# Attention with split values: one product for both halves of v, and part of a weight rounding moved to GpSimd

## The chip, the cores and the metric

The kernel runs on one core of a Trainium2 chip. The metric is the device time of one execution in microseconds (us). Five engines work side by side, each through its own program in order, and wait for each other on semaphores: TensorE (PE, with its weight loads as PEld), VectorE (DVE), ScalarE (ACT), GpSimd (POOL) and SyncE (SP), which issues the transfers.

## What is computed

The reference is one decoder layer on x of shape (16, 256, 512), in three parts, each added to x: attention with 16 heads of width 32, a gated long convolution, and a feed-forward part with weights rounded to 8-bit floats. Cut to what the change touches:

```python
qkv = _bitlinear(layernorm(x), w_qkv)              # int8-like activations, ternary weights
attn = softmax(where(causal, q @ k.T * SCALE, NEG))
out = einsum('bhnm,bmhd->bnhd', attn, v)
x = x + _bitlinear(out, w_proj)                    # out is rounded per row before the product
...
wq = w.astype(float8_e4m3fn).astype(x.dtype)       # gate_w and up_w, 512 x 1536 each
```

## The kernel before, in words

The first part of the program is attention. 16 batches of 8 pairs of heads make 128 pairs, numbered n = 8 b + p. All engines walk the same list of steps t (`STEPS`), and each has its own share of a step, so that pair n is in a different phase on each engine at one time. In step t:

- TensorE first does `weigh(t - 12)` (the product of probabilities and values, L509 to L512), then `row_max(t)` (scores for the row maximum, into the one tile `s_qk`, from L457), then `probabilities(t - 8)` (scores again, into `s_kq`, L478 to L492), and then what projections and transposes are due in that step.
- VectorE first does `take_max(t - 1)` (L802, reads `s_qk`), then now and then `high_part` (L826), `finish` (L834, L838, L844, L847, L852), `scale_qk` (L782), `split_v` (L792, L795), the layer norm's pieces, and last `weight_pieces`.
- ScalarE copies `weigh`'s result out of PSUM into `oraw` (L1216), takes the exponentials (L1202), splits off the high half `pH` (L1208), and rounds.
- GpSimd makes the low half `pL` of the probabilities (L1458), the low halves of q and k (L1451), and its part of `weight_pieces` (L1470, L1473).

There is a single `s_qk`: `row_max(n)` on TensorE waits for `take_max(n - 1)` on VectorE, and `take_max(n)` waits for `row_max(n)`. `pv`, the tile that `weigh` fills, is single too and is freed by ScalarE's copy; `pL` has two buffers, freed by `weigh`.

For precision, probabilities p and values v are each split into two f16 numbers, high and low. A pair has 2 heads and 3 blocks of 128 x 128 each (two on the diagonal, one below). For each block `weigh` issues four products: pH with vH, pH with vL, pL with vL, pL with vH. vH has 33 columns a head (32 values and a column of ones, which gives the softmax sum), vL has 32, and all four add into the same 33 columns of `pv`. That is 24 products a pair, each with a weight load of its own.

Once a batch, `finish` in its step k = 0 takes the reciprocal of the sums (L834) and multiplies `oraw` by it into `o_sb` (L838). Its later steps round and project `o_sb` and add to x.

Beside attention, the 24 pieces (128 x 512) of the gate and up weights are rounded to 8-bit floats, one piece in every five steps. With t % 5 == 1 VectorE masks the exponent of a piece (L865) and turns it into the rounding constant (L867: bound below, then factor), while GpSimd finishes the piece before (L1470). With t % 5 == 0, four steps after the masking, GpSimd adds the constant to the piece (L1473) and VectorE takes a maximum (L871).

After the last pair, the steps run on until the last batch is finished (the tail), x goes through DRAM, and the second part (convolution and feed-forward) begins.

Of the kernel before, what the change touches and what calls it, by code (L numbers as in the profile page):

```python
# [5 lines left out]
F32 = mybir.dt.float32  # L6
F16 = mybir.dt.float16
# [6 lines left out]
P = 128  # L14
# [52 lines left out]
def decoder_kernel(nc, x, skip, ctx_in, w_qkv, w_proj, k_turned, w_gate, w_up, w_down,  # L67
# [23 lines left out]
    with ExitStack() as ctx:  # L91
        def sb(where, name, shape, dt):
            return where.enter_context(nc.sbuf_tensor(name, shape, dt))
# [16 lines left out]
        wmax = sb(ctx, "wmax", [P, 2, CB * INNER // PIECE], F32)  # L110
        cols = sb(ctx, "cols", [P, 2 * IB + M_HEADS], F32)
        gs, us, skips = cols[:, 0:IB], cols[:, IB:2 * IB], cols[:, 2 * IB:]
        rows_s = sb(ctx, "rows_s", [2 * IB, P], F32)
        rows_k = sb(ctx, "rows_k", [M_HEADS, M_POS], F32)
        rows_kb = sb(ctx, "rows_kb", [M_HEADS, B, M_POS], F32)
        same_seq = sb(ctx, "same_seq", [P, B, M_POS], F32)
        GROUP = 4
        ws = sb(ctx, "ws", [P, 8], F32)
# [30 lines left out]
        with ExitStack() as prep:  # L149
            wraw = [sb(prep, f"wraw{i}", [P, WB, C], F32) for i in range(4)]  # L150
            tern = [sb(prep, f"tern{i}", [P, WB, C], BF16) for i in range(2)]
            wsums = sb(prep, "wsums", [P, 4], F32)
        packs.append(q("pack2", [P, 2, R, GQ, N], F16))
        oraw = [q(f"oraw{i}", [P, NT, HEADS, VW], F32) for i in range(2)]
        fw_raw = [q(f"fw_raw{i}", [P, PIECE], F32) for i in range(3)]
        fw_pow = [q(f"fw_pow{i}", [P, PIECE], F32) for i in range(2)]
        o_sb = q("o_sb", [P, NT, C + 1], F32)
        fw_out = [q(f"fw_out{i}", [P, PIECE], F16) for i in range(2)]
        vH = [q(f"vH{i}", [P, NT, HEADS, VW], F16) for i in range(3)]
        vL = [q(f"vL{i}", [P, NT, HEADS, D], F16) for i in range(3)]  # L160
        blockmax = [q(f"blockmax{i}", [P, PAIRS, 6], F32) for i in range(2)]
        negmax = [q(f"negmax{i}", [P, NT, 32], F32) for i in range(2)]
        nmT = [q(f"nmT{i}", [P, N], BF16) for i in range(2)]
# [226 lines left out]
        def tensor_program(tensor):  # L390
# [103 lines left out]

            def weigh(n):
                b, p = divmod(n, PAIRS)
                ph, pl, vh, vl = pH[n % NP], pL[n % 2], vH[b % 3], vL[b % 3]
                acc = pv[:, 0:NT * 2 * VW].rearrange("p (t h w) -> p t h w", t=NT, h=2)
                w.wait_ge(*high_done(n))
                w.wait_ge(low_done, n + 1)  # L500
                w.wait_ge(v_high, 2 * b + 2)
                w.wait_ge(v_low, 2 * b + 2)
                w.wait_ge(const_done, C_ONCE)
                w.wait_ge(pv_out, n)
                for t in range(NT):
                    for hh in range(2):
                        for mt in range(t + 1):
                            block, h = 2 * hh + t if mt == t else 4 + hh, 2 * p + hh
                            T.matmul(acc[:, t, hh, :], ph[:, block, :], vh[:, mt, h, :], start=mt == 0, stop=False)  # L509
                            T.matmul(acc[:, t, hh, 0:D], ph[:, block, :], vl[:, mt, h, :], start=False, stop=False)  # L510
                            T.matmul(acc[:, t, hh, 0:D], pl[:, block, :], vl[:, mt, h, :], start=False, stop=False)
                            made = T.matmul(acc[:, t, hh, :], pl[:, block, :], vh[:, mt, h, :], start=False, stop=mt == t)  # L512
                made.then_inc(pv_pe, 1)

            def turn_oq(b, j):
# [202 lines left out]
        def vector_program(vector):  # L718
# [66 lines left out]
            def split_v(b, t):  # L785
                n, bank = 2 * b + t, misc1.of["v", b, t]
                w.wait_ge(v_pe, n + 1)
                w.wait_ge(c_done, b + 1)
                w.wait_ge(const_done, C_ONCE)
                if b >= 3:  # L790
                    w.wait_ge(pv_pe, PAIRS * (b - 2))
                V.tensor_scalar(vH[b % 3][:, t, :, 0:D], bank[:].rearrange("p (h d) -> p h d", h=HEADS),  # L792
                                small[b % 4][:, 12 + t:13 + t], None, ALU.mult).then_inc(v_high, 1)
                w.wait_ge(v_high, n + 1)
                V.scalar_tensor_tensor(out=vL[b % 3][:, t], in0=bank[:].rearrange("p (h d) -> p h d", h=HEADS),  # L795
                                       scalar=small[b % 4][:, 12 + t:13 + t], in1=vH[b % 3][:, t, :, 0:D],
                                       op0=ALU.mult, op1=ALU.subtract).then_inc(v_low, 1)

            def take_max(n):
# [28 lines left out]
            def finish(b, k):  # L828
# [3 lines left out]
                if k == 0:  # L832
                    w.wait_ge(pv_out, PAIRS * (b + 1))
                    chain.step(V.reciprocal(rl, oraw[b % 2][:, :, :, D]))  # L834
                    chain.wait()
                    if b > 0:
                        w.wait_ge(oqT_pe, 2 * b)
                    V.tensor_tensor(o_sb[:, :, 0:C].rearrange("p t (h d) -> p t h d", d=D), oraw[b % 2][:, :, :, 0:D], rl.unsqueeze(3).broadcast_to([P, NT, HEADS, D]),  # L838
                                    ALU.mult).then_inc(o_mult, 1)
                elif k == 1:  # L840
                    w.wait_ge(o_mult, b + 1)
                    if b >= 2:
                        w.wait_ge(ostep_done, b - 1)
                    V.tensor_reduce(out=am, in_=o_sb[:], op=ALU.max, axis=AXIS.X, apply_absolute_value=True).then_inc(omax_done, 1)  # L844
                elif k == 2:
                    w.wait_ge(ostep_done, b + 1)
                    V.reciprocal(inv, step).then_inc(oscale_done, 1)  # L847
                elif k in (10, 12):
                    t, xs = (k - 10) // 2, x_sb[b % NX]
                    w.wait_ge(proj_pe, 2 * b + t + 1)  # L850
                    w.wait_ge(c2_done, b + 1)
                    V.scalar_tensor_tensor(out=xs[:, t, :], in0=misc1.of["proj", b, t][:], scalar=c2[:, t:t + 1],  # L852
                                           in1=xs[:, t, :], op0=ALU.mult, op1=ALU.add).then_inc(x1_done, 1)

            def weight_pieces(k):
# [3 lines left out]
                if not second and n < PIECES:  # L859
# [2 lines left out]
                    w.wait_ge(fw_in[n % 3], 16 * (n // 3 + 1))  # L862
                    if n >= 2:
                        w.wait_ge(fw_taken, n - 1)
                    chain.step(V.tensor_scalar(pw[:].bitcast(I32), raw[:].bitcast(I32), EXPONENT, None, ALU.bitwise_and))  # L865
                    chain.wait()
                    V.tensor_scalar(pw[:], pw[:], FP8_MIN_NORMAL, FP8_STEP, ALU.max, ALU.mult).then_inc(fw_pow_done, 1)  # L867
                if second and n > 0:
                    m, at = divmod(n - 1, PIECES // 2)
                    w.wait_ge(fw_taken, n)  # L870
# [247 lines left out]
        def scalar_program(scalar):  # L1118
# [90 lines left out]

            def weighed(n):  # L1210
                b, p = divmod(n, PAIRS)
                acc = pv[:, 0:NT * 2 * VW].rearrange("p (t h w) -> p t h w", t=NT, h=2)
                w.wait_ge(pv_pe, n + 1)
                if b >= 2:
                    w.wait_ge(o_mult, b - 1)
# [184 lines left out]
        def gpsimd_program(gpsimd):  # L1400
# [59 lines left out]
            def weight_pieces(k):  # L1460
# [9 lines left out]
                    G.tensor_tensor(fw_out[i % 2][:], fw_raw[i % 3][:], fw_pow[i % 2][:], ALU.subtract).then_inc(fw_taken, 1)  # L1470
                if second and n < PIECES:
                    w.wait_ge(fw_pow_done, n + 1)
                    G.tensor_tensor(fw_raw[n % 3][:], fw_raw[n % 3][:], fw_pow[n % 2][:], ALU.add).then_inc(fw_added, 1)  # L1473

            power_in(0)
# [6 lines left out]
            for i in range(2):  # L1482
                G.memset(nmT[i][:], 0.0).then_inc(const_done, 1)
            for i in range(3):
                G.memset(vH[i][:, :, :, D:VW], 1.0).then_inc(const_done, 1)
            for t in STEPS:
                if (n := pair(t, LOW)) is not None:
                    low_part(n)
# [287 lines left out]
```

## Time and profile before

| what | value |
|---|---|
| median of 3 runs | 1677.63 us (1677.42 to 1678.31) |
| profiled execution | 1676.79 us |
| its span in the trace | 1675.1 us |
| TensorE busy | 1545.5 us (92%) |
| VectorE busy | 1251.7 us (75%) |
| GpSimd busy | 929.1 us (55%) |
| ScalarE busy | 666.0 us (40%) |

The profiled execution is 1.7 us longer than its span and 0.8 us shorter than the median of the runs. The busy shares are averages over parts with different limits: the attention loop takes from 93 us (first `weigh`) to 504 us (last `row_max`) of the span, its tail until about 547 us, the second part the rest. Busy time of TensorE counts each product until its result has drained, so products that follow each other closely overlap in it: starts of products say more than their durations.

### The profile page before, as it was taken

The page shows a single profiled execution, that of the slowest core. Times are in us where ns is not written, and L with a number is a line of the kernel's source. Part 1 is how long each engine was busy: PE and PEld are TensorE (multiplying, and loading weights), DVE is VectorE, ACT ScalarE, POOL GpSimd, SP SyncE. Part 2 cuts the span into 40 slices and gives each one's busy share as a digit, 9 for nine tenths or more (in the row PEclk, how much of TensorE's full clock was granted, in tenths as well). Part 3 has the DMA queues.
Part 4 walks back from the last instruction along what each step waited for, and adds up shares of the span by engine and source line. Part 5 has one row for each costly group of instructions (what it writes and reads, how often), then busy time and mean ns, then how long its engine had stood idle before and what let it go on. Part 6 is the DMA issues. An engine that isn't in the chain of part 4 may idle for free.

```text
span 1675.1 us, 27334 instructions
## 1 busy us (share of the span) xinstructions
PE 1545.5 (92%) x10646; PEld 884.8 (53%) x10646; DVE 1251.7 (75%) x1866; ACT 666.0 (40%) x1190; POOL 929.1 (55%) x677
## 2 busy tenths in 40 slices
PE   2698999999897878899999999999999999999998
PEld 2477777777775333444444444444444444444443
DVE  6799898889883879877777777777776877777521
ACT  4578777777666101322222322222223222232131
POOL 3388788778764455744554545534653454355242
PEclk9799999999998899999999999999999999999999
DMA  3653645545341513010200210020020021010000
GB/s 127 156 135 107 166 108 138 132 114 147 83 112 53 156 44 88 20 32 1 70 26 7 52 38 13 19 70 13 13 76 13 7 64 32 1 45 1 1 26 26
DMA packets 61953, 105.87 MB, mean 63 GB/s; under 512 B 7912, under 2 KB 14080, under 8 KB 61824
## 3 DMA queue, kind: packets, MB, share of 16 engines
q1 hardware_dynamic: 61728, 104.10, 23.5%
q8 instruction: 85, 1.39, 0.3%
q14 instruction: 44, 0.36, 0.1%
q10 hardware_dynamic: 96, 0.01, 0.0%
HBM read 50.61 MB, written 19.92 MB: 42 GB/s over the span
## 4 chain that ended last, share of the span: by engine, by line
PE 75%; DVE 14%; issue 5%; ACT 3%; POOL 1%; DMA 1%; SPq 1%; POOLq 0%; DVEq 0%; ACTq 0%
PE gu L675 20%; PE y L640 11%; PE gu L689 9%; PE gu L628 3%; PE y L643 3%; PE y L648 3%; PE y L647 3%; PE y L644 3%; PE y L646 3%; DVE blockmax L802 3%; PE misc L603 1%; PE s_kq L478 1%; DVE fw_pow L865 1%; PE misc L445 1%; PE misc L436 1%
## 5 line engine op out<-in xcount | busy, mean ns | idle before, releaser
L1539 POOL TENSOR_TENSOR fuL<-fu,fuH 128x512 f16<-128x512 f32 x96 | 116.2, 1210 | 305.5 <-ACT fuH L1356 305.5
L1458 POOL TENSOR_TENSOR pL<-pT,pH 128x768 f16<-128x768 f32 x128 | 220.3, 1723 | 88.5 <-PE pv L512 38.9
L640 PE MATMUL y<-kv,toep 128*128 128x512 f32 x496 | 238.3, 601 | 7.1 <-DVE z L989 6.7
L1000 DVE TENSOR_REDUCE oT<-z 128x64 f32<-128x512 f32 x256 | 175.7, 686 | 8.8
L675 PE MATMUL gu<-fT,wg 128*128 128x512 f16 x768 | 181.4, 379 | 0.0
L675 PE MATMUL gu<-fT,wu 128*128 128x512 f16 x768 | 181.4, 379 | 0.0
L1202 ACT ACTIVATE pT<-s_kq,ws 128x768 f32<-128x768 f32 x128 | 115.3, 901 | 104.1 <-PE s_kq L492 104.1
L1356 ACT ACTIVATE fuH<-fu 128x512 f16<-128x512 f32 x96 | 60.2, 627 | 240.0 <-DVE fu L1016 240.0
L993 DVE TENSOR_TENSOR z<-y,shared 128x512 f32<-128x512 f32 x112 | 77.1, 688 | 95.0 <-PE y L644 60.1
L689 PE MATMUL gu<-wd,fuH 128*128 128x512 f16 x384 | 145.5, 379 | 0.0
L689 PE MATMUL gu<-wd,fuL 128*128 128x512 f16 x384 | 145.5, 379 | 0.0
L1518 POOL TENSOR_TENSOR kv<-vT,cT 128x1024 f32<-128x1024 f32 x64 | 138.5, 2184 | 6.2 <-ACT vT L1333 6.2
L675 PEld LDWEIGHTS gu<-fT,wg 128*128 128x128 f16 x768 | 75.0, 98 | 119.1 <-issue 47.1
L640 PEld LDWEIGHTS y<-kv,toep 128*128 128x128 f32 x496 | 91.5, 192 | 86.9 <-issue 60.0
L996 DVE TENSOR_TENSOR z<-z,cT 128x512 f32<-128x512 f32 x112 | 129.0, 1151 | 3.8
L675 PEld LDWEIGHTS gu<-fT,wu 128*128 128x128 f16 x768 | 75.1, 98 | 106.4 <-issue 35.4
L802 DVE TENSOR_REDUCE blockmax<-s_qk 128x6 f32<-128x768 f32 x128 | 121.4, 948 | 12.0 <-PE s_qk L462 11.7
L1339 ACT ACTIVATE shared<-gu 128x512 f32<-128x512 f32 x56 | 33.4, 597 | 217.1 <-PE gu L628 217.1
L989 DVE TENSOR_TENSOR z<-y,cT 128x512 f32<-128x512 f32 x144 | 98.5, 684 | 28.4 <-PE y L640 28.4
L1451 POOL TENSOR_TENSOR qkhl<-qkt,qkhl 128x512 f16<-128x512 f32 x64 | 80.0, 1252 | 38.5 <-ACT qkhl L1188 38.4
L478 PE MATMUL s_kq<-pack 128*128 128x128 f16 x768 | 100.6, 221 | 0.0
L1016 DVE SCALAR_TENSOR_TENSOR fu<-gu,cols,sil 128x512 f32<-128x512 f32 x96 | 71.5, 745 | 37.6 <-PE gu L675 36.4
(196 smaller groups left out, 3802.0 us busy)
## 6 DMA issues: line engine op xcount, KB each, us to landing
pack<-qkhl SPq DMA_DIRECT2D x256, 128.0 KB, 2.7
x_sb<-in_x SPq DMA_DIRECT2D x16, 512.0 KB, 4.8
c_sb<-in_ctx SPq DMA_DIRECT2D x32, 256.0 KB, 3.9
hankel<-in_L_xattn_k SPq DMA_DIRECT2D x32, 256.0 KB, 4.9
x_grp<-x_scratch SPq DMA_DIRECT2D x32, 256.0 KB, 3.9
out_y<-yo SPq DMA_DIRECT2D x32, 256.0 KB, 2.8
x_scratch<-x_sb SPq DMA_DIRECT2D x15, 512.0 KB, 3.0
wraw<-in_L_attn_w_qkv SPq DMA_DIRECT2D x3, 1024.0 KB, 8.7
```

Of the source, the lines that this page charges most:

```text
L478: T.matmul(to, pack[:, 1, r, g, key * P:(key + 1) * P], pack[:, 0, r, g, query * P:(query + 1) * P], start=first, stop=False)
L640: made = T.matmul(to, tap(h, lb - kb), keys_values(h, kb, half), start=kb == 0, stop=kb == lb)
L675: made = T.matmul(bank[:], (wg, wu)[which][:, cb, ib * P:(ib + 1) * P], fT[:, cb, part, :], start=cb == 0 and part == 0, stop=cb == CB - 1 ...
L689: made = T.matmul(bank[:], src[:, ib, t * P:(t + 1) * P], wd[:, ib, :], start=ib == 0 and part == 0, stop=ib == IB - 1 and part == 1)
L802: V.tensor_reduce(out=blockmax[b % 2][:, p, :], in_=s_qk[:, 0:6, :], op=ALU.max, axis=AXIS.X, negate=True).then_inc(max_done, 1)
L989: V.tensor_tensor(z[n % 2][:], y, weight, ALU.mult).then_inc(m_zm, 1)
L996: chain.step(V.tensor_tensor(z[n % 2][:], z[n % 2][:], weight, ALU.mult))
L1000: V.tensor_reduce(out=oT[h % 2][:, lb, own].rearrange("p (b j) -> p b j", b=HB), in_=z[n % 2][:], op=ALU.add, axis=AXIS.X).then_inc(m_z, 1)
L1202: S.activation(pT[n % NP][:], s_kq[:, 0:6, :], ACT.Exp, scale=ws[:, 4:5]).then_inc(exp_done, 1)
L1458: G.tensor_tensor(pL[n % 2][:], pT[n % NP][:], pH[n % NP][:], ALU.subtract).then_inc(low_done, 1)
L1518: G.tensor_tensor(kv[LB * (h % 2) + lb][:], vT[h % 2][:, lb, :].rearrange("p (b i) -> p b i", b=B).unsqueeze(2).broadcast_to([P, B, M_POS, ...
L1539: G.tensor_tensor(fuL[:, ib, :], fu[n % 2][:], fuH[:, ib, :], ALU.subtract).then_inc(f_fl, 1)
```

## The change

vH and vL become one tile `vHL` with 65 columns a head: 32 high values, the column of ones, 32 low values. `weigh` issues two products a block instead of four: pH with all 65 columns, pL with all 65 columns, into 65 columns of `pv`. ScalarE's copy into `oraw` takes 260 elements instead of 132. `finish` adds the last 32 columns of each head to the first 32, once a batch, between the reciprocal and the multiplication. The second step of the weight pieces' constant (L867) goes from VectorE to GpSimd, where it stands ahead of the addition L1473. Three small tiles move into a region of memory that is used again later.

```diff
-        oraw = [q(f"oraw{i}", [P, NT, HEADS, VW], F32) for i in range(2)]
+        oraw = [q(f"oraw{i}", [P, NT, HEADS, VW + D], F32) for i in range(2)]
-        vH = [q(f"vH{i}", [P, NT, HEADS, VW], F16) for i in range(3)]
-        vL = [q(f"vL{i}", [P, NT, HEADS, D], F16) for i in range(3)]
+        vHL = [q(f"vHL{i}", [P, NT, HEADS, VW + D], F16) for i in range(3)]
...
-                            T.matmul(acc[:, t, hh, :], ph[:, block, :], vh[:, mt, h, :], start=mt == 0, stop=False)
-                            T.matmul(acc[:, t, hh, 0:D], ph[:, block, :], vl[:, mt, h, :], start=False, stop=False)
-                            T.matmul(acc[:, t, hh, 0:D], pl[:, block, :], vl[:, mt, h, :], start=False, stop=False)
-                            made = T.matmul(acc[:, t, hh, :], pl[:, block, :], vh[:, mt, h, :], start=False, stop=mt == t)
+                            T.matmul(acc[:, t, hh, :], ph[:, block, :], v[:, mt, h, :], start=mt == 0, stop=False)
+                            made = T.matmul(acc[:, t, hh, :], pl[:, block, :], v[:, mt, h, :], start=False, stop=mt == t)
...
                     chain.step(V.reciprocal(rl, oraw[b % 2][:, :, :, D]))
+                    chain.step(V.tensor_tensor(oraw[b % 2][:, :, :, 0:D], oraw[b % 2][:, :, :, 0:D], oraw[b % 2][:, :, :, VW:VW + D],
+                                               ALU.add))
                     chain.wait()
...
-                    chain.step(V.tensor_scalar(pw[:].bitcast(I32), raw[:].bitcast(I32), EXPONENT, None, ALU.bitwise_and))
-                    chain.wait()
-                    V.tensor_scalar(pw[:], pw[:], FP8_MIN_NORMAL, FP8_STEP, ALU.max, ALU.mult).then_inc(fw_pow_done, 1)
+                    V.tensor_scalar(pw[:].bitcast(I32), raw[:].bitcast(I32), EXPONENT, None, ALU.bitwise_and).then_inc(fw_pow_done, 1)
...
                     w.wait_ge(fw_pow_done, n + 1)
+                    chain.step(G.tensor_scalar(fw_pow[n % 2][:], fw_pow[n % 2][:], FP8_MIN_NORMAL, FP8_STEP, ALU.max, ALU.mult))
+                    chain.wait()
                     G.tensor_tensor(fw_raw[n % 3][:], fw_raw[n % 3][:], fw_pow[n % 2][:], ALU.add).then_inc(fw_added, 1)
```

## Rows read from the trace of the kernel before

**Rows 1.** The page: span of the profiled execution.

```profile
span 1675.1 us, 27334 instructions
```

**Rows 2.** Stretches: PE, PEld, DVE, ACT, POOL busy us, then granted clock.

```profile
93.00:504.00 411.00, 373.91 (x5677) 312.15 (x5676) 367.31 (x557) 307.72 (x620) 329.50 (x235) 0.98 0.48 123
504.00:547.00 43.00, 29.82 (x445) 21.39 (x443) 15.19 (x23) 25.15 (x49) 18.24 (x11) 0.85 0.20 66
...
700.00:1675.00 975.00, 967.62 (x3808) 457.18 (x3806) 675.44 (x985) 257.64 (x397) 458.51 (x316) 1.00 0.10 28
```

**Rows 3.** Who waited for whom, 93 to 505 us: total us, times, longest.

```profile
PE s_qk L457 <- DVE blockmax L802: 32.9, 26, 2.6
...
DVE vH L792 <- PE misc L445: 13.0, 19, 0.8
```

**Rows 4.** TensorE in order of time around 325 us: start us, us, engine, line.

```profile
324.24 0.22 PE L478 MATMUL s_kq<-pack 128*128 128x128 f16 x1
...
324.35 0.22 PE L478 MATMUL s_kq<-pack 128*128 128x128 f16 x1
...
325.34 0.18 PE L509 MATMUL pv<-vH,pH 128*128 128x33 f16 x1
...
325.92 0.18 PE L512 MATMUL pv<-vH,pL 128*128 128x33 f16 x1
```

**Rows 5.** VectorE groups by line, 90 to 533 us: count, busy us, mean ns.

```profile
L867 DVE TENSOR_SCALAR fw_pow<-fw_pow 128x512 f32<-128x512 f32 x22 | 27.5, 1252 | 0.8
...
L838 DVE TENSOR_TENSOR o_sb<-oraw,osmall 128x1024 f32<-128x1024 f32 x16 | 24.2, 1515 | 0.8 <-PE misc L521 0.3
```

**Rows 6.** VectorE L838 alone: min/median/max ns.

```profile
L838 DVE TENSOR_TENSOR o_sb<-oraw,osmall x16: 1226/1253/2299, 122.9 to 532.0; 128x1024 f32<-128x1024 f32 x16
```

**Rows 7.** What TensorE waited for before L509: us, times.

```profile
  POOL pL L1458: 0.5, 1
```

**Rows 8.** GpSimd in order of time around 320 us.

```profile
319.99 1.65 POOL L1458 TENSOR_TENSOR pL<-pT,pH 128x768 f16<-128x768 f32 x1 [0.26 <-PE pv L512]
```

**Rows 9.** GpSimd's part of the rounding: min/median/max ns.

```profile
L1473 POOL TENSOR_TENSOR fw_raw<-fw_raw,fw_pow x24: 1265/1275/1287, 69.1 to 483.4; 128x512 f32<-128x512 f32 x24
```

**Rows 10.** ScalarE copies out of PSUM, 132 and 256 elements: min/median/max ns.

```profile
L1216 ACT ACTIVATE oraw<-pv x128: 253/272/322, 94.7 to 531.0; 128x132 f32<-128x132 f32 x128
...
L1160 ACT ACTIVATE cbc<-misc x16: 375/376/384, 25.6 to 435.1; 128x256 f32<-128x256 f32 x16
```

**Rows 11.** TensorE in order of time: L457 of pairs 68 to 72.

```profile
293.01 0.38 PE L457 MATMUL s_qk<-pack 128*128 128x256 f16 x2
...
295.91 0.38 PE L457 MATMUL s_qk<-pack 128*128 128x256 f16 x2
...
299.04 0.38 PE L457 MATMUL s_qk<-pack 128*128 128x256 f16 x2
...
302.81 0.38 PE L457 MATMUL s_qk<-pack 128*128 128x256 f16 x2
...
308.16 0.41 PE L457 MATMUL s_qk<-pack 128*128 128x256 f16 x2 [2.29 <-DVE blockmax L802]
```

**Rows 12.** VectorE in order of time, the same stretch.

```profile
294.49 0.95 DVE L802 TENSOR_REDUCE blockmax<-s_qk 128x6 f32<-128x768 f32 x1
...
297.55 0.94 DVE L802 TENSOR_REDUCE blockmax<-s_qk 128x6 f32<-128x768 f32 x1
...
301.19 0.95 DVE L802 TENSOR_REDUCE blockmax<-s_qk 128x6 f32<-128x768 f32 x1
...
305.49 1.75 DVE L867 TENSOR_SCALAR fw_pow<-fw_pow 128x512 f32<-128x512 f32 x1
307.16 0.94 DVE L802 TENSOR_REDUCE blockmax<-s_qk 128x6 f32<-128x768 f32 x1
```

**Rows 13.** TensorE in order of time: L457 of pairs 42 and 82.

```profile
199.09 0.39 PE L457 MATMUL s_qk<-pack 128*128 128x256 f16 x2 [1.41 <-DVE blockmax L802]
...
346.00 0.39 PE L457 MATMUL s_qk<-pack 128*128 128x256 f16 x2 [1.42 <-DVE blockmax L802]
```

More of the change, by code:

```diff
@@ L112, in decoder_kernel @@
         gs, us, skips = cols[:, 0:IB], cols[:, IB:2 * IB], cols[:, 2 * IB:]
-        rows_s = sb(ctx, "rows_s", [2 * IB, P], F32)
-        rows_k = sb(ctx, "rows_k", [M_HEADS, M_POS], F32)
-        rows_kb = sb(ctx, "rows_kb", [M_HEADS, B, M_POS], F32)
         same_seq = sb(ctx, "same_seq", [P, B, M_POS], F32)
@@ L152, in decoder_kernel @@
             wsums = sb(prep, "wsums", [P, 4], F32)
+            rows_s = sb(prep, "rows_s", [2 * IB, P], F32)
+            rows_k = sb(prep, "rows_k", [M_HEADS, M_POS], F32)
+            rows_kb = sb(prep, "rows_kb", [M_HEADS, B, M_POS], F32)
         packs.append(q("pack2", [P, 2, R, GQ, N], F16))
-        oraw = [q(f"oraw{i}", [P, NT, HEADS, VW], F32) for i in range(2)]
+        oraw = [q(f"oraw{i}", [P, NT, HEADS, VW + D], F32) for i in range(2)]
         fw_raw = [q(f"fw_raw{i}", [P, PIECE], F32) for i in range(3)]
@@ L496, in weigh @@
                 b, p = divmod(n, PAIRS)
-                ph, pl, vh, vl = pH[n % NP], pL[n % 2], vH[b % 3], vL[b % 3]
-                acc = pv[:, 0:NT * 2 * VW].rearrange("p (t h w) -> p t h w", t=NT, h=2)
+                ph, pl, v = pH[n % NP], pL[n % 2], vHL[b % 3]
+                acc = pv[:, 0:NT * 2 * (VW + D)].rearrange("p (t h w) -> p t h w", t=NT, h=2)
                 w.wait_ge(*high_done(n))
@@ L791, in split_v @@
                     w.wait_ge(pv_pe, PAIRS * (b - 2))
-                V.tensor_scalar(vH[b % 3][:, t, :, 0:D], bank[:].rearrange("p (h d) -> p h d", h=HEADS),
+                V.tensor_scalar(vHL[b % 3][:, t, :, 0:D], bank[:].rearrange("p (h d) -> p h d", h=HEADS),
                                 small[b % 4][:, 12 + t:13 + t], None, ALU.mult).then_inc(v_high, 1)
                 w.wait_ge(v_high, n + 1)
-                V.scalar_tensor_tensor(out=vL[b % 3][:, t], in0=bank[:].rearrange("p (h d) -> p h d", h=HEADS),
-                                       scalar=small[b % 4][:, 12 + t:13 + t], in1=vH[b % 3][:, t, :, 0:D],
+                V.scalar_tensor_tensor(out=vHL[b % 3][:, t, :, VW:VW + D], in0=bank[:].rearrange("p (h d) -> p h d", h=HEADS),
+                                       scalar=small[b % 4][:, 12 + t:13 + t], in1=vHL[b % 3][:, t, :, 0:D],
                                        op0=ALU.mult, op1=ALU.subtract).then_inc(v_low, 1)
@@ L1211, in weighed @@
                 b, p = divmod(n, PAIRS)
-                acc = pv[:, 0:NT * 2 * VW].rearrange("p (t h w) -> p t h w", t=NT, h=2)
+                acc = pv[:, 0:NT * 2 * (VW + D)].rearrange("p (t h w) -> p t h w", t=NT, h=2)
                 w.wait_ge(pv_pe, n + 1)
@@ L1484, in gpsimd_program @@
             for i in range(3):
-                G.memset(vH[i][:, :, :, D:VW], 1.0).then_inc(const_done, 1)
+                G.memset(vHL[i][:, :, :, D:VW], 1.0).then_inc(const_done, 1)
             for t in STEPS:
```

## The prediction

> **What bounds the kernel now.** I read the page first for the span [rows 1], then the busy time of each engine in four stretches [rows 2]. The change touches only attention and the weight rounding beside it, so only the loop (93 to 504 us) and its tail count; of the second part the reader should see that TensorE is busy 967.6 of 975 us, and nothing of it is edited. I take it as unchanged: whatever attention gains or loses passes to the end in full.
>
> In the loop no engine is full: TensorE 373.9, VectorE 367.3, GpSimd 329.5 and ScalarE 307.7 of 411 us. The third view, who waited for whom, says how the first two share the time [rows 3]: TensorE's scores (L457) waited 32.9 us in 26 places for VectorE's maximum (L802), since there is one `s_qk`, while VectorE's own largest wait for TensorE is the 13.0 us ahead of L792. So the limit alternates. In most of the steps TensorE runs without a gap, in about a quarter VectorE is late and TensorE stands. A gain on one engine is worth something only in its own steps.
>
> **TensorE's part.** The 24 products of a pair start from 325.34 to 325.92, with 23 intervals between them: 25 ns each, 0.605 us a pair [rows 4]. The change issues 12. The trace has no 65-column product. Bounds: no cheaper than the 33 columns' 25 ns (12 x 25 = 0.30 us), no dearer than 128 columns, where two products take from 324.24 to 324.35, 55 ns each [rows 4] (12 x 55 = 0.66 us, slightly more than now). Per column the 128-column row gives 0.43 ns, so 65 columns want 28 ns; I take 28, since 25 ns at 33 columns lies above that line and so looks like a floor that 65 columns only just pass. 12 x 28 = 0.34 us: TensorE saves 0.27 us a pair, and could save 0.30 or lose 0.05.
>
> The Trainium skill, "TensorE: Matmul & The Clock Gate", section "Back-to-back issue gap", speaks against this: it gives a sustained spacing of about 81 ns a product at 128 columns for a stream of weight load and product, because both set the pace. If 65 columns cost that, a pair would take 0.97 us instead of 0.605, an estimate from that page. The trace has 55 ns there, so I go by the trace; the rule is taken up below as a rival.
>
> The first twelve steps of scores have no `weigh` beside them; 116 pairs have both. If TensorE alone set the time, 116 x 0.27 = 31 us would go.
>
> **VectorE's part.** Removed: L867, mean 1.25 us in the loop [rows 5], 24 of them, 30 us. That is far more than the instruction's own work must be, but it stands in VectorE's queue all the same. Added: 16 additions, of the shape of L838 (1024 elements, two inputs in SBUF): 1.23 us at least, 1.52 on the mean, 2.30 at most [rows 5, 6]. I take 1.23 plus 0.04 for the chained wait in the walk below, and charge the difference to the mean, 0.29, separately. 16 x 1.5 = 24 us. So VectorE's total hardly changes (30 off, 24 on); what changes is in which steps it stands. The removed piece lies in steps n % 5 == 1, VectorE's longest, where TensorE's waits are. The added piece lies in the step where a batch finishes. Behind it on VectorE stand L838, L782 and the next L802, for which TensorE waits.
>
> **Both together, step by step.** Two facts of the rows make a walk possible [rows 11, 12]: a released L457 starts 1.00 us after the L802 it waited for (307.16 to 308.16), and otherwise follows its own queue. Write P for TensorE's own work between two L457 and D for VectorE's between two L802. Pairs 68 to 72, before: P = 2.90, 3.13, 3.77, and 5.35 less the 2.29 that it waited and the 0.15 by which a product's drain (0.18) outlasts the next start, so 2.91; D = 3.06 (with L838), 3.64, 5.97 (with L867 at 1.75) [rows 11, 12]. After: each P less 0.27; the first D plus 1.27, the last less 1.75: 4.33, 3.64, 4.22. Start both as they stand, L457 of pair 68 at 0, L802 at 1.48:
>
> - pair 69: L457 at 2.63, L802 at 5.81.
> - pair 70: L457 at max(5.49, 6.81) = 6.81 (a new wait of 1.3), L802 at 9.45.
> - pair 71: L457 at max(10.31, 10.45) = 10.45, L802 at 13.67.
> - pair 72: L457 at max(13.09, 14.67) = 14.67 (a wait of 1.5, before 2.29).
>
> Before it was 15.15: four steps give 0.5 us where TensorE alone saves 1.1. The addition takes back what the removal gives. The pattern of batches (8 steps) and pieces (5 steps) repeats after 40 pairs, from pair 42 at 199.09 to pair 82 at 346.00, 146.9 us [rows 13]. Walked in the same way, its eight groups of five give 0.8, 2.5, 0.5, 1.0, 0.9, 1.1, 1.2 and -0.3 us: 7.7 us. The groups with a finish give 0.6 on the mean, those without 1.5. In steps with `split_v` the saving is also partly lost, as VectorE waits there for TensorE's v, and the shorter `weigh` comes after it. For 116 pairs: 116 / 40 x 7.7 = 22 us.
>
> **What is taken off this.** Additions that meet GpSimd work: 15 in the loop at 0.29 more, 4 us, of which I count 3, since some of these steps have slack. The tail: ScalarE is busy 25.2 of 43 us there, and has the exponentials and copies in a row. Its copy grows from 132 to 260 elements, 272 to 376 ns by the 256-element row [rows 10], 0.1 us a pair: hidden in the loop (ScalarE idles 103 us there), 1.2 us in the tail's 12 steps. The last batch's addition has no cover, since everything waits for `o_sb`: 1.3 us. No instruction and no transfer is added to SP's queue.
>
> **GpSimd's part.** Added: 24 times one 128 x 512 instruction. The trace has no such instruction with a single input. The two-input one of that size, 1.28 us [rows 9], is the upper bound; VectorE's L867 at its mean, 1.25, is no better. A gain is excluded, as work is only added, so the lower end is zero; I take 1.0, near the upper row, 24 us in all, or 350 of 390 us busy. What covers it: `pL` is ready early. The one that the `weigh` at 325.34 uses ended at 319.99 + 1.65 = 321.64, 3.7 us ahead [rows 4, 8], and TensorE waited for `pL` once in the whole execution, 0.5 us [rows 7]. Four steps lie between VectorE's masking and GpSimd's use of it, so the new place makes nobody wait. Cost 0. With that cover gone (less than 1 us of lead left) each piece could stop TensorE by up to 1.28, 31 us.
>
> Sum: 22 - 3 - 1.2 - 1.3 = 16.5 us off the profiled 1676.8, 1660.3; the median stands 0.8 higher, so **1661 us**.
>
> **Rivals.** First, *the freed time comes out nearly whole*: VectorE's waits for TensorE shrink with `weigh`, and the walk charges the addition too high. For it: the removed L867 sits where TensorE waits. Against: the walk. 31 - 2.5 = 29 us, 1648.
>
> Second, *the addition takes it all*: it meets GpSimd instructions as the longest L838 did, at 2.30, nearly every time, now that GpSimd is fuller. 15 x 1.1 = 16 us against the 3 that I charged, a gain of 4: about 1673, or no measurable change. For it: 2.30 exists. Against: the median is 1.25 [rows 6].
>
> Third, the other side, *the wide product is dear*. Its place is TensorE in `weigh`, its price the spacing of 65-column products with a weight load each; TensorE loses from 50 ns a product on. At 55 ns it costs 116 x 0.05 = 6 us, which the removal of L867 about balances (24 waits shortened by a part of 1.25, 16 lengthened). At 75 ns it would be 12 x 75 - 605 = 0.3 us a pair, 34 us, less some 5: 1706. For it speaks only that two instructions issue per product; against it the 55 ns at 128 columns. By the page's 81 ns it would be 0.37 a pair, some 43 us, near 1715.
>
> **How the numbers follow.** A measurement of this kernel can tell about 0.2%, 3.4 us, from no change. Forecast (1653 to 1669): 0.60. Nearly whole gain (1645 to 1653): 0.19. Addition takes it: 0.17, of which 0.07 is no measurable change. Wide product dear: 0.04. Faster 0.60 + 0.19 + 0.10 = 0.89, same 0.07, slower 0.04. The range goes from 1646 to 1672: the lower end holds most of the second case with 0.30 us a pair, the upper the larger half of the third.
>
> **What would show it.** Right: 12 products a pair from first to last in 0.3 to 0.35 us; the loop's 411 us become about 393; TensorE's waits for L802 stay at some 25 to 35 us, but some stand behind the steps with a finish; the addition at 1.2 to 1.6 us; the tail 2 us longer; the second part as long as before. Wrong: products more than 40 ns apart, waits of TensorE for `pL` of more than a few us, additions near 2.3, or TensorE's waits falling below 15 us (then the gain is larger).

## The result and the profile after

The changed kernel takes 1686.72 us (median of 4 runs, 1685.04 to 1687.05), the kernel before 1677.97 on the same chip: a ratio of 1.0049, 95% interval 1.0032 to 1.0067. It is slower by 8.7 us; 1661 was predicted. One execution of a later kernel, the one with the multiplication moved, took 2052.81 us at a granted clock of 0.74, in a slower state of the chip, and is left out of its median. Page and stretches of the changed kernel (columns as in [rows 2]; the loop is cut from the row maximum of pair 12 to that of pair 127, the second stretch ends at the first product of the second part):

```profile
span 1683.2 us, 24212 instructions
```

```profile
95.00:507.60 412.60, 349.41 (x4192) 282.14 (x4249) 372.15 (x544) 317.74 (x616) 383.44 (x256) 0.97 0.47 121
507.60:555.70 48.10, 27.39 (x297) 19.21 (x300) 20.07 (x28) 27.31 (x50) 18.76 (x12) 0.85 0.22 70
555.70:1683.20 1127.50, 1097.22 (x4172) 515.89 (x4172) 803.73 (x1182) 285.60 (x438) 544.34 (x376) 0.99 0.13 34
```

The same three stretches of the kernel before:

```profile
97.00:504.00 407.00, 371.21 (x5631) 309.79 (x5630) 363.35 (x552) 305.65 (x616) 327.24 (x233) 0.98 0.48 122
504.00:549.40 45.40, 29.82 (x445) 21.40 (x444) 15.81 (x27) 25.96 (x50) 18.80 (x12) 0.83 0.24 74
549.40:1675.00 1125.60, 1094.49 (x4172) 514.35 (x4172) 803.94 (x1182) 285.58 (x438) 544.82 (x376) 0.99 0.13 34
```

The ramp before the loop became 2.0 us shorter, the loop 5.6 longer, the tail 2.7 longer, the second part 1.9 longer: together, but for rounding, the 8.1 us between the spans. Why the ramp and the second part changed by 2 us each is not shown. In the loop TensorE is busy 22 us less, as intended. VectorE is busy 8.8 us more, although it was meant to lose as much as it gained, and GpSimd 56 us more.

Where this comes from. TensorE's products, in order of time:

```profile
322.24 0.19 PE L509 MATMUL pv<-vHL,pH 128*128 128x65 f16 x1
322.27 0.20 PE L510 MATMUL pv<-vHL,pL 128*128 128x65 f16 x1
...
322.61 0.38 PE L457 MATMUL s_qk<-pack 128*128 128x256 f16 x2
```

Twelve products in 0.37 us, 31 ns each, where 24 had started 25 ns apart [rows 4]: the price was nearly right. VectorE's finish and GpSimd's rounding, minimum, median and maximum in ns:

```profile
L833 DVE TENSOR_TENSOR oraw<-oraw x16: 1160/1514/2454, 121.1 to 535.4; 128x1024 f32<-128x1024 f32 x16
L838 DVE TENSOR_TENSOR o_sb<-oraw,osmall x16: 1227/2547/2556, 123.2 to 536.6; 128x1024 f32<-128x1024 f32 x16
```

```profile
L1471 POOL TENSOR_SCALAR fw_pow<-fw_pow x24: 1917/1922/2782, 68.6 to 483.6; 128x512 f32<-128x512 f32 x24
L1473 POOL TENSOR_TENSOR fw_raw<-fw_raw,fw_pow x24: 1261/1272/1452, 70.7 to 485.6; 128x512 f32<-128x512 f32 x24
```

The addition's median is 1.51 us, and L838, which the change does not touch, went from a median of 1.25 [rows 6] to 2.55. GpSimd's new instruction takes 1.92 us, more than the two-input instruction of the same size that was my upper bound [rows 9]. The waits between 93 and 505 us, where [rows 3] had 32.9 us for TensorE:

```profile
ACT pT L1200 <- POOL pL L1456: 43.3, 32, 2.9
...
PE s_qk L457 <- DVE blockmax L800: 35.6, 25, 3.5
PEld pv L509 <- issue: 29.5, 46, 2.8
```

TensorE waits for VectorE as long as before, although VectorE has lost L867, and ScalarE now waits 43.3 us for `pL`, for which only TensorE had waited, once, before [rows 7]: an exponential needs a `pT` that GpSimd has read. The last line, in which the profile names no releaser, hides a wait of the same kind. In 16 places of attention TensorE stands for more than 0.3 us, 13.9 us together, and then starts `weigh` 0.10 us after GpSimd's L1456 has ended; in the kernel before there is no such place. GpSimd's line and TensorE's, where the addition L833 (268.94 to 270.45) had held up L1456:

```profile
269.32 2.63 POOL L1456 TENSOR_TENSOR pL<-pT,pH 128x768 f16<-128x768 f32 x1
```

```profile
272.05 0.19 PE L509 MATMUL pv<-vHL,pH 128*128 128x65 f16 x1 [0.45 <-issue]
```

### The profile page after: what moved, and what is told of

Same layout as the page of the kernel before. It is cut to its first block, busy times and chain, and to the rows that moved or that the text cites. A ratio compares the mean times of both kernels' runs of the same rounds, so it can differ in the third digit from the quotient of the medians.

```text
span 1683.2 us, 24212 instructions
## 1 busy us (share of the span) xinstructions
PE 1520.8 (90%) x9044; PEld 854.9 (51%) x9110; DVE 1263.3 (75%) x1858; ACT 679.3 (40%) x1190; POOL 988.2 (59%) x701
## 4 chain that ended last, share of the span: by engine, by line
PE 76%; DVE 11%; issue 6%; ACT 4%; POOL 2%; DMA 1%; POOLq 0%; SPq 0%; DVEq 0%; ACTq 0%
PE gu L673 20%; PE y L638 11%; PE gu L687 9%; PE gu L626 3%; PE y L641 3%; PE y L646 3%; PE y L645 3%; PE y L642 3%; PE y L644 3%; DVE blockmax L800 2%; PE s_kq L478 2%; PE misc L445 2%; PE misc L436 1%; PE misc L601 1%; PE s_qk L457 1%
## 5 line engine op out<-in xcount | busy, mean ns | idle before, releaser
L1456 POOL TENSOR_TENSOR pL<-pT,pH 128x768 f16<-128x768 f32 x128 | 227.8, 1787 | 31.6 <-ACT pH L1206 19.2
L1200 ACT ACTIVATE pT<-s_kq,ws 128x768 f32<-128x768 f32 x128 | 115.5, 902 | 86.5 <-POOL pL L1456 43.3
L800 DVE TENSOR_REDUCE blockmax<-s_qk 128x6 f32<-128x768 f32 x128 | 121.3, 948 | 12.9 <-PE s_qk L462 12.3
L1449 POOL TENSOR_TENSOR qkhl<-qkt,qkhl 128x512 f16<-128x512 f32 x64 | 81.8, 1280 | 35.1 <-ACT qkhl L1186 35.1
```

The costliest lines, as they stand in the source:

```text
L800: V.tensor_reduce(out=blockmax[b % 2][:, p, :], in_=s_qk[:, 0:6, :], op=ALU.max, axis=AXIS.X, negate=True).then_inc(max_done, 1)
L1200: S.activation(pT[n % NP][:], s_kq[:, 0:6, :], ACT.Exp, scale=ws[:, 4:5]).then_inc(exp_done, 1)
L1456: G.tensor_tensor(pL[n % 2][:], pT[n % NP][:], pH[n % NP][:], ALU.subtract).then_inc(low_done, 1)
```

## The experiments

**Two halves, and the addition alone.** Four kernels, timed together. The first keeps the wide products and the addition and puts the constant back on VectorE:

```diff
 # against the changed kernel, VectorE
-                    V.tensor_scalar(pw[:].bitcast(I32), raw[:].bitcast(I32), EXPONENT, None, ALU.bitwise_and).then_inc(fw_pow_done, 1)
+                    chain.step(V.tensor_scalar(pw[:].bitcast(I32), raw[:].bitcast(I32), EXPONENT, None, ALU.bitwise_and))
+                    chain.wait()
+                    V.tensor_scalar(pw[:], pw[:], FP8_MIN_NORMAL, FP8_STEP, ALU.max, ALU.mult).then_inc(fw_pow_done, 1)
 # GpSimd
-                    chain.step(G.tensor_scalar(fw_pow[n % 2][:], fw_pow[n % 2][:], FP8_MIN_NORMAL, FP8_STEP, ALU.max, ALU.mult))
-                    chain.wait()
```

> The values' half of the change alone: 65-column products and the addition once a batch; bound and factor stay on VectorE. Theory G (GpSimd's new 1.92 us instruction is what failed): faster than the kernel before by 5 to 12 us, ScalarE's wait for pL (43 us in the changed kernel) gone. Theory A (the added addition on VectorE, with GpSimd in between, is what failed): no better than before, 1678 to 1690 us, L838 still near 2.5 us.

The second is the kernel before with the opposite of this edit, and so the rounding's half alone:

> The rounding's half alone: bound and factor on GpSimd, products and finish as before. Theory G: slower than before by 3 to 12 us, with ScalarE waiting for pL. Theory A: faster by 5 to 15 us, since VectorE loses 30 us from its longest steps.

The third and the fourth are the first and the whole change, each without the addition, so that the result leaves out the low half of v:

```diff
-                    chain.step(V.tensor_tensor(oraw[b % 2][:, :, :, 0:D], oraw[b % 2][:, :, :, 0:D], oraw[b % 2][:, :, :, VW:VW + D],
-                                               ALU.add))
```

> As the values' half alone, but without the addition, so the low part of v is left out of the result. It prices the addition: Theory G puts it at 3 to 8 us for 16 of them (the rest of the gain is kept), Theory A at 15 us or more, more than its own 25 us of busy time would suggest after slack, with L838 back at a median of 1.25 us.

> The whole change without the addition (the low part of v is left out of the result). Theory G: still held by GpSimd, 1675 us or more. Theory A: most of the loss is gone, 1655 to 1665 us.

| kernel | us | ratio to before, 95% interval |
|---|---|---|
| wide products and addition | 1711.65 | 1.0199 (1.0186 to 1.0212) |
| rounding on GpSimd alone | 1660.88 | 0.9894 (0.9880 to 0.9908) |
| wide products, no addition | 1675.53 | 0.9982 (0.9971 to 0.9994) |
| whole change, no addition | 1656.99 | 0.9872 (0.9859 to 0.9884) |

The third kernel's twelve executions spread from 1667.63 to 1679.64, far wider than any other's. Of the two theories, A fits the signs of all four, and G fails on all four. A's sizes were missed in three places: the first kernel is 22 us above its range of 1678 to 1690, the second gained 17.1 us where 5 to 15 were expected, and L838's median in the third is 1.42 us, not 1.25. The addition costs 36.1 us where the rounding is on VectorE (1711.65 less 1675.53) and 29.7 where it is on GpSimd (1686.72 less 1656.99). Moving the constant brings 17.1 us alone, in spite of GpSimd's 1.92. Halving the products brings next to nothing: 2.4 us without the move, 3.9 with it (1660.88 less 1656.99). The loops of the first three, in this order:

```profile
97.10:534.50 437.40, 360.37 (x4192) 292.91 (x4249) 389.33 (x566) 319.44 (x616) 335.72 (x233) 0.93 0.44 113
```

```profile
96.70:487.00 390.30, 363.02 (x5563) 303.87 (x5629) 347.90 (x531) 305.40 (x616) 371.64 (x256) 1.00 0.51 128
```

```profile
99.40:503.00 403.60, 345.11 (x4195) 283.88 (x4252) 364.62 (x550) 317.27 (x616) 327.31 (x233) 0.98 0.48 123
```

**Is the addition dear because TensorE has less to do?** With fewer products TensorE idles longer, and in the first kernel above its granted clock is 0.93 in the loop. The kernel before, with its 24 narrow products, got the addition as well:

```diff
-        oraw = [q(f"oraw{i}", [P, NT, HEADS, VW], F32) for i in range(2)]
+        oraw = [q(f"oraw{i}", [P, NT, HEADS, VW + D], F32) for i in range(2)]
...
+                    chain.step(V.tensor_tensor(oraw[b % 2][:, :, :, 0:D], oraw[b % 2][:, :, :, 0:D], oraw[b % 2][:, :, :, VW:VW + D],
+                                               ALU.add))
...
+            for i in range(2):
+                chain.step(V.memset(oraw[i][:, :, :, VW:VW + D], 0.0))
```

> The kernel before, four products a block, plus the addition of the changed kernel (it adds columns of zeros). If the addition's price is VectorE's alone: 1700 to 1715, 25 to 35 us more than before, as between the two kernels with wide products (1675.5 and 1711.7). If it is that high only because TensorE, with half of the products gone, idles longer and falls to its lower clock: 1685 to 1695.

1710.97 us, ratio 1.0191 (1.0176 to 1.0206): the addition costs 32 us here too. With it in place, 12 wide products (1711.65, at a granted clock of 0.93 in the loop) and 24 narrow ones (1710.97, at 0.97) take the same time. These two alone could hide a saving of the products behind a cost of the clock. The pairs without the addition do not: there the clocks are equal (0.98 and 0.98, 1.00 and 1.00), and the products still bring only 2.4 and 3.9 us. So the clock is not what eats TensorE's saving. Its loop and its finish:

```profile
99.90:533.90 434.00, 377.48 (x5631) 312.61 (x5629) 387.27 (x565) 307.75 (x616) 332.88 (x233) 0.97 0.45 115
```

```profile
L835 DVE TENSOR_TENSOR oraw<-oraw x16: 1156/1279/2398, 125.7 to 561.5; 128x1024 f32<-128x1024 f32 x16
L840 DVE TENSOR_TENSOR o_sb<-oraw,osmall x16: 1226/2546/2556, 127.1 to 562.7; 128x1024 f32<-128x1024 f32 x16
```

VectorE is busy 23.9 us more than before, of which the 14 additions in the loop are 14 x 1.54 = 21.6 and the longer L840 (the old L838) 10.8, while the two steps of the rounding's constant got 8.2 shorter; the loop is 27 us longer.

**What a plain microsecond of VectorE costs.** A reduction with one input in the addition's place, its result unused:

```diff
+                    chain.step(V.tensor_reduce(out=spare[:, 0:NT], in_=oraw[b % 2][:, :, :, 0:D],
+                                               op=ALU.max, axis=AXIS.XY))
```

> The kernel before with one more VectorE instruction in each batch's finish, in the place of the addition: a reduction with a single input and about 1.2 us long, whose result nobody uses. If VectorE's time counts one to one: loop longer by 14 times 1.2 us and the whole by 16 to 21 us, 1694 to 1700, with L838 still 1.5 us on the mean. If the addition cost 32 us only because of the port that it shares with GpSimd, and a plain microsecond of VectorE has slack: less than 10 us, below 1688.

1689.79 us, ratio 1.0067 (1.0053 to 1.0081): 11 us, between the two expectations.

```profile
96.90:513.20 416.30, 367.69 (x5563) 309.67 (x5629) 372.83 (x565) 306.98 (x616) 327.02 (x233) 0.98 0.47 120
```

```profile
L836 DVE TENSOR_REDUCE spare<-oraw x16: 1152/1160/1162, 122.7 to 541.0; 128x2 f32<-128x1024 f32 x16
L841 DVE TENSOR_TENSOR o_sb<-oraw,osmall x16: 1226/1676/2275, 123.9 to 542.2; 128x1024 f32<-128x1024 f32 x16
```

The 14 reductions in the loop are 16.2 us, yet VectorE's busy time rose by only 9.5, and the loop by 9.3. So here busy time passed one to one, but the length of what is added does not predict it: the two steps of the rounding's constant got 9.4 us shorter together, and L841 (the old L838) 3.1 longer. They probably meet GpSimd at other moments.

The loop's length less VectorE's busy time in it is 44 us before, 40 after, 48, 42, 39 and 47 in the four experiments' loops above, 43 here, and between 36 and 48 in those below, while the busy time itself goes from 342 to 389 and the loop from 381 to 437. That is a strong correlation, but 12 us of play is more than what the halved products bring, so it does not rank the engines in any single kernel.

**Why L838 doubled.** The finish in the changed kernel's step of pair 69, first VectorE and then GpSimd, in order of time:

```profile
298.20 0.95 DVE L800 TENSOR_REDUCE blockmax<-s_qk 128x6 f32<-128x768 f32 x1
...
299.32 1.33 DVE L833 TENSOR_TENSOR oraw<-oraw 128x1024 f32<-128x1024 f32 x1
300.69 2.55 DVE L838 TENSOR_TENSOR o_sb<-oraw,osmall 128x1024 f32<-128x1024 f32 x1
...
303.83 0.93 DVE L800 TENSOR_REDUCE blockmax<-s_qk 128x6 f32<-128x768 f32 x1
```

```profile
300.21 1.94 POOL L1456 TENSOR_TENSOR pL<-pT,pH 128x768 f16<-128x768 f32 x1 [0.64 <-ACT pH L1206]
302.11 2.14 POOL L1449 TENSOR_TENSOR qkhl<-qkt,qkhl 128x512 f16<-128x512 f32 x1
```

GpSimd's L1456 begins inside the addition (299.32 to 300.65), takes 1.94 us instead of the usual 1.65, and ends at 302.15. L838 begins at 300.69 and ends at 303.24, 1.1 us after L1456's end: about its own length of 1.23, counted from there. L1449, begun at 302.11, takes 2.14 us instead of 1.16 in its turn. So the two engines take turns: the addition holds up GpSimd's next instruction, and that one holds up L838. The Trainium skill, page "SBUF — State Buffer", section "Who interferes with whom", has this as a rule: a VectorE instruction with two SBUF inputs contends with a GpSimd instruction that reads SBUF, and the port pair that they share is an exclusive lock. The trace agrees, and over all finishes. In 12 of the 16 of the changed kernel L838 takes over 2 us; in each of them a two-input instruction of GpSimd is running when it starts, and L838 ends 1.08 or 1.09 us after that one's end. The same 1.08 us holds for the three long ones of the kernel before: its maximum of 2.30 [rows 6] starts at 475.18, and L1458 runs from 474.75 to 476.40. Where GpSimd runs nothing at the start, L838 takes 1.23. The two finishes at 1.52 meet GpSimd's L1471, which has one input, and end before it does: that one is not waited for to its end.

What the addition changes is how often this happens, 12 times in 16 instead of 3. That GpSimd is fuller does not explain it: in the kernel before plus the addition GpSimd is busy 332.9 us of the loop, hardly more than the 327.2 before, and L840's mean there is 2.29 us; with the rounding alone GpSimd is busy 371.6 and L838's mean is 1.78.

Two tests. First, the addition as two reductions with a single input each, before the multiplication:

```diff
-                    chain.step(V.tensor_tensor(oraw[b % 2][:, :, :, 0:D], oraw[b % 2][:, :, :, 0:D], oraw[b % 2][:, :, :, VW:VW + D],
-                                               ALU.add))
+                    for t in range(NT):
+                        part = bass.AP(tensor=src.tensor, offset=src.offset + t * HEADS * (VW + D),
+                                       ap=[src.ap[0], [VW + D, HEADS], [1, D], [VW, 2]])
+                        chain.step(V.tensor_reduce(out=o_out[:, t], in_=part, op=ALU.add, axis=AXIS.X))
```

> The whole change, with the addition done as two single-input reductions over pairs (high, low) of 512 results each, into o_sb, which is then multiplied in place. Theory L (the two-input addition and multiplication let one waiting GpSimd instruction in between them and stand still for it): L838 falls from a median of 2.55 us back to a mean near 1.5 us, although VectorE's own work grows by about 1 us; time within 6 us of the changed kernel, 1680 to 1692. Theory W (only VectorE's added work counts, wherever GpSimd stands): L838 stays above 2.2 us and the time rises above 1695.

1693.24 us, ratio 1.0084 (1.0069 to 1.0099), and the multiplication:

```profile
L842 DVE TENSOR_TENSOR o_sb<-o_sb,osmall x16: 1226/1858/2594, 124.5 to 549.5; 128x1024 f32<-128x1024 f32 x16
```

```profile
96.00:519.50 423.50, 361.07 (x4250) 287.51 (x4248) 376.01 (x557) 318.79 (x616) 368.76 (x256) 0.95 0.45 117
```

Inconclusive: a median of 1.86 us is neither the 1.5 of theory L nor the 2.2 of theory W, and the time lies between the two expectations. Shorter than 2.55, but the two reductions take 2.4 us, 0.8 more than the addition, and more than eat that up. A neighbour with one input does not keep GpSimd out of L842's way either: its long cases, up to 2.59 us, again end 1.08 us after a GpSimd instruction that was running at their start.

Second, the multiplication moved by one step, so that other work stands between:

```diff
                     chain.step(V.tensor_tensor(oraw[b % 2][:, :, :, 0:D], oraw[b % 2][:, :, :, 0:D], oraw[b % 2][:, :, :, VW:VW + D],
                                                ALU.add))
+                elif k == 1:
                     chain.wait()
...
-                elif k == 1:
                     w.wait_ge(o_mult, b + 1)
```

> The whole change, with the multiplication L838 moved from the finish's step 0 to its step 1, so that a maximum (L800) and other VectorE work stand between it and the addition. If L838's 2.55 us in the changed kernel come from one GpSimd instruction that the addition held up and that then takes the port at the addition's end: L838's mean falls to 1.5 to 1.8 us, VectorE's busy time in the loop by 7 to 12 us, and the time with it, 1674 to 1680. If L838 is long because GpSimd is fuller in general: L838's mean stays above 2.1 us and the time at 1683 to 1690.

1685.22 us, ratio 1.0045 (1.0033 to 1.0058): nothing that can be told from the whole change at 1.0049. The numbers of the second expectation came out, a mean of L838 above 2.1 us (2.18 over all 16) and a time in 1683 to 1690; its reason, that GpSimd is fuller in general, is answered above. The timeline shows another:

```profile
332.69 1.16 DVE L833 TENSOR_TENSOR oraw<-oraw 128x1024 f32<-128x1024 f32 x1
333.77 0.68 DVE L780 TENSOR_TENSOR qkt<-misc,cbc 128x512 f32<-128x512 f32 x1
...
335.30 0.54 DVE L824 CAST pH<-pT 128x768 f16<-128x768 f32 x1
335.77 2.67 DVE L839 TENSOR_TENSOR o_sb<-oraw,osmall 128x1024 f32<-128x1024 f32 x1
```

```profile
96.20:512.10 415.90, 354.03 (x4198) 284.73 (x4254) 375.42 (x544) 318.83 (x616) 387.57 (x256) 0.96 0.47 120
```

In step 1 of the finish VectorE has its cast L824 just ahead of the multiplication (L839 now), in 15 of 16 finishes. In 13 of them a GpSimd instruction that began during the cast still runs when L839 starts (L1456 takes 1.95 to 2.04 us there instead of 1.65), and L839 takes 2.18 to 2.67 us. The new place has a second price: L780 stands behind the multiplication, and TensorE now waits for it, where it had waited 1.5 us (between 96 and 512 us):

```profile
PE misc L436 <- DVE qkt L780: 26.7, 11, 3.4
```

So the place was badly chosen. A kernel in which the addition and the multiplication both stand apart from every instruction that shares the port was not tried.

**GpSimd's price.** With the factor alone on GpSimd (weights below the smallest step are then rounded too finely), a single run:

> The rounding's half alone, with the factor but without the bound on GpSimd (weights below the smallest normal step are rounded too finely). It prices GpSimd's instruction: if its two operations cost one pass each, 1.92 us falls to 1.0 to 1.3 us; if the instruction costs by the element whatever it does, it stays above 1.8 us.

```profile
L1471 POOL TENSOR_SCALAR fw_pow<-fw_pow x24: 1489/1497/2484, 68.8 to 459.4; 128x512 f32<-128x512 f32 x24
```

1.50 us instead of 1.92: a second operation costs 0.42, and neither expectation holds. The single run took 1654.12 us, 7 below the kernel with both, which is one run and no interval. Then the constant on ScalarE, from the kernel before (the larger of x and m, times s, is relu(s x - s m) + s m):

```diff
+            def weight_constant(k):
+                ...
+                if not second and n < PIECES:
+                    pw = fw_pow[n % 2]
+                    w.wait_ge(fw_pow_done, n + 1)
+                    S.activation(pw[:], pw[:], ACT.Relu, bias=kmin[:, 0:1], scale=FP8_STEP).then_inc(fw_relu, 1)
+                    w.wait_ge(fw_relu, n + 1)
+                    S.activation(pw[:], pw[:], ACT.Copy, bias=FP8_MIN_NORMAL * FP8_STEP).then_inc(fw_const, 1)
```

> The kernel before with bound and factor on ScalarE, as two instructions of about 0.6 us a piece (a relu with scale and bias, then a bias), one step after the masking. If GpSimd's 1.92 us costs time (ScalarE's 45 us of waits for pL in the kernel with the rounding alone): 1650 to 1657, below 1660.9. If ScalarE's queue is no cheaper a place, or the waits for pL cost nothing: 1659 to 1668.

1654.90 us, ratio 0.9851 (0.9835 to 0.9867). It is 6.0 us below the kernel with the constant on GpSimd (1660.88), as the first expectation had it; the two were timed on different chips, and by their ratios, each to the kernel before beside it, it is 7.2:

```profile
L1263 ACT ACTIVATE fw_pow<-fw_pow,kmin x24: 705/718/742, 70.0 to 453.6; 128x512 f32<-128x512 f32 x24
L1265 ACT ACTIVATE fw_pow<-fw_pow x24: 629/630/632, 70.8 to 454.3; 128x512 f32<-128x512 f32 x24
```

```profile
96.40:481.40 385.00, 365.04 (x5630) 304.41 (x5629) 341.51 (x530) 329.26 (x658) 323.61 (x233) 1.00 0.52 130
```

**TensorE once more.** Three narrow products a block instead of four, pL with vL left out, once with the constant on GpSimd and once on ScalarE:

```diff
-                            T.matmul(acc[:, t, hh, 0:D], pl[:, block, :], vl[:, mt, h, :], start=False, stop=False)
```

> Bound and factor on GpSimd, narrow products, pL with vL left out (18 products a pair instead of 24): TensorE saves 0.15 us a pair and VectorE gets no addition. If TensorE's saving is worth little while VectorE sets the pace: 1657 to 1661, as without any saving (1660.9). If VectorE's relief has made TensorE the bound: 1645 to 1655.

> Bound and factor on ScalarE and three narrow products a block (pL with vL left out). If VectorE's busy time sets the loop one to one (loop time less VectorE's busy time was 39 to 48 us in all nine kernels so far), TensorE's 0.15 us a pair brings little more: 1649 to 1655 against 1654.9 with four products. If TensorE has become the bound now that VectorE is relieved: 1638 to 1646.

1656.44 us (0.9866, 0.9851 to 0.9881) and 1650.69 us (0.9834, 0.9821 to 0.9847). Each is some 4 us below its twin with four products (1660.88 and 1654.90); by the ratios to the kernels before beside them, 4.7 and 2.9. The first lies 0.6 us below the range for a saving that is worth little, in the gap to the other, and the second inside that range. TensorE's saving of 0.15 us a pair would be 17 us. The last is the fastest kernel of the study, with the low-order product pL vL missing; 1654.90 is the fastest that computes all that the kernel before does.

```profile
95.30:476.10 380.80, 347.57 (x4885) 288.44 (x4940) 344.44 (x529) 329.44 (x658) 323.60 (x233) 1.00 0.52 131
```

**Could it be GpSimd that sets the pace?** In the kernels with the constant on GpSimd this engine is the fullest: 371.64 of 390.30 us (95%) with the rounding alone, 383.44 of 412.60 (93%) in the changed kernel. TensorE waits for its `pL` there, as the rows of the changed kernel show, and without the addition still in 23 places, 17.6 us. So in them the small worth of halved products is no proof for VectorE. Where GpSimd has room, busy 80 to 85% of the loop, it is small too: 2.4 us for the wide products on the kernel before, some 3 or 4 for three products instead of four with the constant on ScalarE; in that last pair there is no wait for `pL` of over 0.3 us.

## Why the prediction was wrong

The step that failed is "Both together, step by step", in both of its terms.

**VectorE's part: the addition.** I put 1.27 us into a finish step and 0.29 on the mean for meeting GpSimd. Pair 68 to 69 shows it whole: the walk had D = 4.33 us, the rows above have 303.83 - 298.20 = 5.63, the addition 1.33 and L838 2.55 where it was 1.23 [rows 12]. So the addition takes 0.1 us more than in the walk and L838 1.3 more; over the loop the mean of the 14 is 2.28 us instead of 1.52. TensorE's released product shows the consequence, a wait that was none before [rows 11]:

```profile
299.30 0.38 PE L457 MATMUL s_qk<-pack 128*128 128x256 f16 x2
...
304.82 0.39 PE L457 MATMUL s_qk<-pack 128*128 128x256 f16 x2 [2.48 <-DVE blockmax L800]
```

I had the row for it, the maximum of 2.30 [rows 6], and used it as a rival ("the addition takes it all"), but as a chance that would strike at random; with the addition ahead of it L838 meets a running GpSimd instruction in most finishes. Measured, the addition costs 30 to 36 us, against some 22 of VectorE's time that the walk (15 x 1.27) and its correction (3) charged.

**TensorE's part: what 0.27 us a pair is worth.** Its size was right (31 ns a product, not 28, so 0.23 us a pair); its worth was not. I subtracted it from each P and let it move VectorE's next instruction. In the kernel with wide products and no addition TensorE's wait for L800 rose instead, from 32.9 us [rows 3] to

```profile
PE s_qk L457 <- DVE blockmax L800: 47.8, 33, 3.6
```

and two stretches of VectorE show why. The kernel before, and that kernel, from one maximum through `split_v` to the second after it:

```profile
198.09 0.95 DVE L802 TENSOR_REDUCE blockmax<-s_qk 128x6 f32<-128x768 f32 x1
...
199.85 0.96 DVE L802 TENSOR_REDUCE blockmax<-s_qk 128x6 f32<-128x768 f32 x1 [0.35 <-PE s_qk L462]
...
202.04 0.75 DVE L792 TENSOR_SCALAR vH<-misc,small 128x512 f16<-128x512 f32 x1 [0.78 <-PE misc L445]
...
203.50 0.95 DVE L802 TENSOR_REDUCE blockmax<-s_qk 128x6 f32<-128x768 f32 x1
```

```profile
199.64 0.95 DVE L800 TENSOR_REDUCE blockmax<-s_qk 128x6 f32<-128x768 f32 x1
...
201.41 0.96 DVE L800 TENSOR_REDUCE blockmax<-s_qk 128x6 f32<-128x768 f32 x1 [0.35 <-PE s_qk L462]
...
203.59 0.75 DVE L790 TENSOR_SCALAR vHL<-misc,small 128x512 f16<-128x512 f32 x1 [0.79 <-PE misc L445]
...
205.05 0.95 DVE L800 TENSOR_REDUCE blockmax<-s_qk 128x6 f32<-128x768 f32 x1
```

5.41 us in both. VectorE releases the scores, TensorE computes scores and v, VectorE splits v: `weigh` is not on that round: TensorE does it after v and ahead of the next scores, which wait for VectorE anyway. This is one round of many, but the sum over the loop agrees: VectorE's wait for v is 13.0 us before [rows 3] and 12.5 there. I had named this ("in steps with `split_v` the saving is also partly lost") and undercharged it. TensorE saves 27 us of products over the loop (116 x 0.23), but its wait for VectorE grew by about 15, and the loop became only 3.4 us shorter. The profile before did not tell which engine decides: they were busy 91% and 89% of the loop. I took the number of steps in which TensorE runs without a gap for the number in which it decides, but a TensorE that was fed by VectorE a step earlier looks just as full.

**The removal of L867** was right in sign and too large in size. 30 us of VectorE's time were forecast, of which 27.1 stood in the loop; the loop's busy time fell by 15.5 and the time by 17.1, since L838, the cast L826 and the masking L865 became 11.6 us longer together. **GpSimd's part** was forecast at no cost, from an upper bound of 1.28 us. It takes 1.92. The `pL` lead of 3.7 us was no measure: ScalarE waits for the same instruction through `pT`, and TensorE came to wait for `pL` in 16 places, 13.9 us, which the prediction had named as a sign of being wrong. The kernel with the constant on ScalarE puts this cost at 6 to 7 us. **The tail** was forecast 2.5 us longer and is 2.7.

None of the three rivals came as written. The slower one needed a wide product dearer than 50 ns, and it takes 31. The second came nearest, "the addition takes it all", but dearer than I had priced it and beside a TensorE gain of nearly nothing: by the medians, +30 for the addition, -17 for the move, -4 for the products, 9 us slower.

Three things stay open: how long L838 would be in a place away from every instruction that shares the port; why the loop keeps some 40 us in which VectorE stands, which no run set out to shorten; and how the changed kernel's loss divides between VectorE and the waits for `pL`, since the addition lengthens L1456 too.

## What to carry to other kernels

When two engines are both about nine tenths busy and feed each other, their busy shares do not tell which one sets the pace; find that out, by adding a known instruction to each, before pricing an edit. Follow one whole round between them and see which instructions are on it, since work outside the round can be halved for nothing. In this kernel an elementwise VectorE instruction with two SBUF inputs, put right ahead of another of its kind, cost more than its own length, for GpSimd took a turn in between; price the pair, not the instruction. And a reversed comparison, the kernel before plus the one added instruction, would have priced the addition in one run, at 32 us where 22 were charged.

## What the runs showed of the hardware

- One GpSimd instruction on 128 x 512 f32 with one input and two constants takes 1.92 us, with one constant 1.50, while the addition of two tensors of that size takes 1.27: one input is not cheaper than two here.
- Products of 65 columns with a weight load each start 31 ns apart, those of 33 columns 25, of 128 columns 55.
- VectorE's multiplication (two SBUF inputs, 128 x 1024 f32) takes 1.23 us alone. Begun while a two-input instruction of GpSimd runs, it ends 1.08 or 1.09 us after that one's end, up to 2.67 us in all (kernels before and changed, and the one with the multiplication moved). VectorE's single-input reduction of the same tile took 1.15 to 1.16 us in all 16 finishes.
- A busy share of 90% on two engines did not tell the limit: TensorE's busy time in the loop fell by 22 to 26 us with the wide products, and the kernels without the addition gained 2.4 and 3.9 us.
- ScalarE's two passes over 128 x 512 f32 from and to SBUF took 0.72 and 0.63 us.
